# A place of its own for every gathered and result tile in the last stage of an expert layer, with deeper buffers around it

## What is computed

```python
gate_scores = softmax(x @ Wg.T)                      # x: 2048 tokens of 256
topk_val, topk_idx = top_k(gate_scores, 2)
topk_val = topk_val / (topk_val.sum() + EPS)
for e in range(8):
    a, b = split(x @ W1[e].T + b1[e])                # 2 x 512
    g = a * sigmoid(b)
    out = out + (g @ Wo.T + bo) * comb[..., e]       # comb: 2 of the 8 are not zero
x = x + out
```

## Time and profile before

| | us |
|---|---|
| runs without profile: median of 3 | 633.45 (632.12 to 635.2) |
| the profiled execution, its own time | 636.3 |
| its span, first to last instruction | 634.4 |
| first gather of the combination issued at | 569.75 |
| last addition begins at | 630.90 |

### The profile page before, as it was taken

How to read it: one execution, slowest core, us unless ns; L and a number is a source line. 1 busy time by engine, 2 the same in 40 slices (tenths; PEclk the granted TensorE clock), 3 DMA queues, 4 the chain that set the end, 5 groups by cost and what they waited for, 6 DMA issues and landing times. The chain is left out here.

```text
span 634.4 us, 21694 instructions
## 1 busy us (share of the span) xinstructions
PE 599.9 (95%) x8364; PEld 487.6 (77%) x8364; DVE 459.2 (72%) x1073; ACT 339.9 (54%) x743; POOL 330.7 (52%) x482
## 2 busy tenths in 40 slices
PE   9999999999999999999999999886999999997677
PEld 4788878888788887888886788663678888864456
DVE  3688867887778886777775855888799877763343
ACT  3677867888687886887772446441322333321111
POOL 3357858688587885788852332130422332207560
PEclk9999999999999999999999999896999999999798
DMA  9624644857255746965203991039334434427672
GB/s 244 148 67 108 185 153 123 240 164 226 93 190 162 209 134 190 232 186 168 72 3 105 429 368 34 34 112 385 126 126 136 139 125 137 129 93 208 165 227 63
DMA packets 65204, 102.10 MB, mean 161 GB/s; under 512 B 15408, under 2 KB 42096, under 8 KB 64080
## 3 DMA queue, kind: packets, MB, share of 16 engines
q1 hardware_dynamic: 59808, 86.42, 42.3%
q0 software_dynamic: 4432, 13.50, 7.7%
q10 hardware_dynamic: 864, 0.79, 0.5%
HBM read 69.42 MB, written 31.26 MB: 159 GB/s over the span
## 5 line engine op out<-in xcount | busy, mean ns | idle before, releaser
L537 DVE TENSOR_SCALAR Pm<-scores 128x514 f32<-128x514 f32 x128 | 88.1, 688 | 57.0 <-PE scores L750 56.8
L653 ACT ACTIVATE Pm<-Pm,nm 128x257 f32<-128x257 f32 x256 | 115.8, 505 | 2.5 <-DVE nm L542 2.5
L542 DVE TENSOR_REDUCE nm<-Pm 128x2 f32<-128x514 f32 x128 | 87.5, 684 | 2.2
L1634 POOL DMA_INDIRECT Xg<-y_d,inv x39 | 37.1, 951 | 87.2 <-PE scores L1819 69.9
L648 ACT ACTIVATE PT<-bank 128x512 f32<-128x512 f32 x64 | 38.2, 598 | 74.3 <-PE bank L761 74.3
L731 PE MATMUL bank<-hA,wH 128*128 128x258 f32 x256 | 75.4, 305 | 0.1
L738 PE MATMUL bank<-wH,hA 128*128 128x256 f32 x256 | 74.5, 302 | 0.5 <-DVE PT L549 0.5
L761 PE MATMUL bank<-cst,Pm 128*128 128x128 f32 x512 | 69.9, 279 | 0.0
L731 PE MATMUL bank<-hA,wL 128*128 128x258 f32 x256 | 69.1, 280 | 0.0
L738 PE MATMUL bank<-wL,hA 128*128 128x256 f32 x256 | 68.9, 280 | 0.0
L1834 PE MATMUL bank<-W,xh 128*128 x208 | 66.7, 402 | 1.0 <-DVE xl L1742 1.0
(11 more groups left out here) (262 smaller groups left out, 1449.2 us busy)
## 6 DMA issues: line engine op xcount, KB each, us to landing
w_d<-whl SPq DMA_DIRECT2D x64, 256.0 KB, 3.5
W<-w_d SPq DMA_DIRECT2D x8, 2048.0 KB, 15.5
g_d<-gg SPq DMA_DIRECT2D x39, 256.0 KB
wst<-in_W1T SPq DMA_DIRECT2D x32, 256.0 KB, 3.5
cx<-in_ctxT SPq DMA_DIRECT2D x31, 258.0 KB, 3.0
cx<-in_ctxT SPq DMA_DIRECT2D x62, 129.0 KB, 3.4
bb<-in_b SPq DMA_DIRECT2D x8, 512.0 KB
xb<-in_x SPq DMA_DIRECT2D x4, 512.0 KB, 4.6
```

The source lines that it names most:

```text
L537: v.tensor_scalar(Pm[:, i % 2, 2 * p:2 * p + 2, :], S4[:, 2 * p:2 * p + 2, 0:NK], -CLAMP, CLAMP, ALU.max, ALU.min).then_inc(s_cl, 1)
L542: v.tensor_reduce(nm[:, i % 2, 2 * p:2 * p + 2], Pm[:, i % 2, 2 * p:2 * p + 2, :], AX.X, ALU.max, negate=True).then_inc(s_nm, 1)
L653: a.activation(Pm[:, i % 2, g, :], Pm[:, i % 2, g, :], ACT.Exp, bias=nm[:, i % 2, g:g + 1]).then_inc(s_ex, 1)
L1634: g.indirect_dma_start(out=Xg[:, i % 3, :], out_offset=None, in_=y_d, in_offset=bass.IndirectOffsetOnAxis(ap=inv[:, i:i + 1], axis=0)).the ...
```

## The change

`cg` and `fo` get a place for each of the 16 tiles, and `zc` and `zT` get four in place of two. They lie where the expert weights were, which the first gather waits for in both kernels. The waits follow the new sizes:

```diff
-        area(27, 60)
-        cg = put("cg", [128, 4, 2, 512])
-        zc = put("zc", [128, 2, 512])
-        zT = put("zT", [128, 2, 512])
-        fo = put("fo", [128, 4, C])
+        area(27, 155)
+        cg = put("cg", [128, NTILE, 2, 512])
+        zc = put("zc", [128, 4, 512])
+        zT = put("zT", [128, 4, 512])
+        fo = put("fo", [128, NTILE, C])
...
                     if j >= 4:
-                        g.wait_ge(c_z, j - 3)
+                        g.wait_ge(c_g[j % 4], 32 * (j // 4))
...
             def final(v, j):
                 v.wait_ge(c_o, j + 1)
-                if j >= 4:
-                    v.wait_ge(c_out[j % 4], 32 * (j // 4))
...
-                    if j >= 2:
-                        v.wait_ge(c_t, j - 1)
+                    if j >= 4:
+                        v.wait_ge(c_t, j - 3)
...
-                    if j >= 2:
-                        final(v, j - 2)
-                final(v, NTILE - 2)
-                final(v, NTILE - 1)
+                    if j >= 4:
+                        final(v, j - 4)
+                for j in range(NTILE - 4, NTILE):
+                    final(v, j)
...
-                    if j >= 2:
-                        a.wait_ge(c_o, j - 1)
-                    a.activation(zT[:, j % 2, :], B[j % 2][:, :], ACT.Copy).then_inc(c_te, 1)
+                    if j >= 4:
+                        a.wait_ge(c_o, j - 3)
+                    a.activation(zT[:, j % 4, :], B[j % 4][:, :], ACT.Copy).then_inc(c_te, 1)
...
                 def back(j):
                     t.wait_ge(c_z, j + 1)
-                    if j >= 2:
-                        t.wait_ge(c_te, j - 1)
+                    if j >= 4:
+                        t.wait_ge(c_te, j - 3)
...
                 back(0)
+                back(1)
                 for j in range(NTILE):
-                    if j + 1 < NTILE:
+                    if j < NTILE - 4:
+                        back(j + 2)
+                    if NTILE - 4 < j < NTILE - 1:
                         back(j + 1)
```

More of the change, by code:

```diff
@@ L1622, in _ @@
                     for b in range(2):
-                        sp.dma_start(od[j, b], fo[64 * b:64 * b + 64, j % 4, :]).then_inc(c_out[j % 4], 16)
+                        sp.dma_start(od[j, b], fo[64 * b:64 * b + 64, j, :]).then_inc(c_out[j % 4], 16)
                 for s in c_out:
@@ L1642, in _ @@
                     if j >= 4:
-                        g.wait_ge(c_z, j - 3)
+                        g.wait_ge(c_g[j % 4], 32 * (j // 4))
                     for k in range(2):
-                        g.indirect_dma_start(out=cg[:, j % 4, k, :], out_offset=None, in_=g_d,
+                        g.indirect_dma_start(out=cg[:, j, k, :], out_offset=None, in_=g_d,
                                              in_offset=bass.IndirectOffsetOnAxis(ap=pi[:, k, j:j + 1], axis=0)
@@ L1671, in final @@
                 v.wait_ge(c_o, j + 1)
-                if j >= 4:
-                    v.wait_ge(c_out[j % 4], 32 * (j // 4))
-                v.tensor_tensor(fo[:, j % 4, :], B[4 + j % 4][:, 0:C], xb[:, j, :], ALU.add).then_inc(c_f, 1)
+                v.tensor_tensor(fo[:, j, :], B[4 + j % 4][:, 0:C], xb[:, j, :], ALU.add).then_inc(c_f, 1)
             @block.vector
@@ L1756, in _ @@
                     v.wait_ge(c_g[j % 4], 32 * (j // 4 + 1))
-                    if j >= 2:
-                        v.wait_ge(c_t, j - 1)
-                    v.tensor_scalar(zc[:, j % 2, :], cg[:, j % 4, 0, :], cmb[:, 0, j:j + 1], None, ALU.mult
+                    if j >= 4:
+                        v.wait_ge(c_t, j - 3)
+                    v.tensor_scalar(zc[:, j % 4, :], cg[:, j, 0, :], cmb[:, 0, j:j + 1], None, ALU.mult
                                     ).then_inc(c_m, 1)
                     v.wait_ge(c_m, j + 1)
-                    v.scalar_tensor_tensor(out=zc[:, j % 2, :], in0=cg[:, j % 4, 1, :], scalar=cmb[:, 1, j:j + 1],
-                                           in1=zc[:, j % 2, :], op0=ALU.mult, op1=ALU.add).then_inc(c_z, 1)
-                    if j >= 2:
-                        final(v, j - 2)
-                final(v, NTILE - 2)
-                final(v, NTILE - 1)
+                    v.scalar_tensor_tensor(out=zc[:, j % 4, :], in0=cg[:, j, 1, :], scalar=cmb[:, 1, j:j + 1],
+                                           in1=zc[:, j % 4, :], op0=ALU.mult, op1=ALU.add).then_inc(c_z, 1)
+                    if j >= 4:
+                        final(v, j - 4)
+                for j in range(NTILE - 4, NTILE):
+                    final(v, j)
             @block.scalar
@@ L1841, in back @@
                     t.wait_ge(c_z, j + 1)
-                    if j >= 2:
-                        t.wait_ge(c_te, j - 1)
+                    if j >= 4:
+                        t.wait_ge(c_te, j - 3)
                     for m in range(4):
-                        mm = t.transpose(B[j % 2][:, 128 * m:128 * m + 128], zc[:, j % 2, 128 * m:128 * m + 128], ident)
+                        mm = t.transpose(B[j % 4][:, 128 * m:128 * m + 128], zc[:, j % 4, 128 * m:128 * m + 128], ident)
                     mm.then_inc(c_t, 1)
@@ L1861, in _ @@
                     for m in range(4):
-                        mm = t.matmul(B[4 + j % 4][:, 0:C], zT[:, j % 2, 128 * m:128 * m + 128], WoT[:, m, :],
+                        mm = t.matmul(B[4 + j % 4][:, 0:C], zT[:, j % 4, 128 * m:128 * m + 128], WoT[:, m, :],
                                       start=(m == 0), stop=(m == 3))
```

## The result

The change makes the kernel slower: a median of 648.25 us (646.74 to 650.83, 4 runs) against 634.33 us (632.12 to 635.70, 4 runs) for the kernel before in the same comparison, a ratio of 1.0209 with a 95% interval of 1.0172 to 1.0246. The forecast was 623.5 and the range 619.5 to 631. It is rival D that came about: its span of 645.4 was met to within a microsecond, its time of 644.5 was 3.8 us under the median. The profiled execution took 646.74 us, the least of the four, with a span of 644.8.

A forecast was written before the change was run, and what follows sets the result against it. POOL's issue of gathers was taken as the slowest step, interrupted by waits for sums that late PE ends delayed. From 636.3 profiled, -12.9 + 3.0 = -9.9 gave 626.4, and 2.9 lower for plain runs 623.5 us; range 619.5 to 631.

The forecast's parts named there:

- rival D: Running gathers keep PE's ends back from about product 1 until 612.5; slower, 644.5 us; chance 0.13.
- Holds that stay: Late PE ends remain after the change, behind more buffers; cost +3.0 us at the end, with 0 and 6.5 as ends.
- holds: Ends of PE's work reaching other engines late, after PE's row ends; about 8.9 us at product 1, 4.0 at copy 11.
- the sum: Forecast total: end 12.9 us earlier, plus 3.0, makes -9.9 from the profiled 636.3; plain runs 2.9 lower, 623.5 us.
- The gathers' part: On POOL, the landing wait costs nothing and 32 gathers run without a gap; last issue ends 6.9 us earlier.
- The argument from the profiler: Plain runs' median is only 2.9 us below the profiled execution, so the late PE ends were taken as real.
- A: No late PE ends left, or none showing at the end: -12.9 us, 620.5 us; chance 0.25.
- B: Gather and store transfers become the bound, 240 or 213 GB/s: 622.5 to 628 us; chance 0.10 of over 627.5.
- C: Late PE ends grow with the unbroken run of gathers, eating most of the gain: 630 to 636 us; chance 0.09.
- Additions four behind: On DVE, addition j-4 behind sum j costs nothing more, with 0.9 us free for each tile.
- transpositions two ahead: On PE, product j stands behind transposition j+2 and ends a tile later; the later addition covers it, at no price.
- The slow start: After a pause PE runs at a lower clock, so its first product costs up to 1.7 us more.

The follow-up runs named there:

- e9: Changed kernel with POOL writing 256-float-wide zeros to unused SBUF behind each gather and waiting for it; 636.66 us, ratio 1.0009.
- e1: Changed kernel with the old wait put back: tile j's gathers wait for the sum of tile j-4; 636.32 us, ratio 1.0012.
- e3: Changed kernel with the 32 gathers replaced by plain transfers of consecutive rows issued by SP, same bytes; 618.12 us, one execution.
- e14: Changed kernel with each product cut into two halves of 128 columns, doubling its matrix instructions; 650.11 us, one run.
- e11: Changed kernel with POOL writing 16-float-wide zeros to unused SBUF behind each gather and waiting for it; 640.20 us, ratio 1.0039.

## Why the prediction was wrong

**The step that failed** is "Holds that stay": it took +3.0 us, with ends at 0 and 6.5. Without holds the sum's span is 634.4 - 12.9 = 621.5; the measured span is 644.8, so by the sum's own terms the holds cost 23.3. The gathers' part came true: 32 gathers without a gap, the last begun at 609.04 (near 609 forecast), the landing wait never binding, landings not slower (sum 5, the last sum that is not behind a held addition, begins at 587.43). The rest of the 12.9 the result can't test, as the holds cover it. The runs without holds put it a little lower: in e9 the end comes 13.8 us behind the begin of the last gather (621.40, span 635.2), where the sum had 621.5 - 608.9 = 12.6; by that the span without holds would be near 622.8 and the holds cost 22.

**Why it was taken too small.** I read the lengths of the holds, 9 and 4 us, as a property of PE that the change leaves alone ("The change takes none away; it puts more buffers behind them"). They were the lengths at which POOL's stop, or its last gather, had ended them. In the kernel before a hold makes a sum late, the late sum stops POOL (4.65 us), and the stop lets PE's ends through. e1 shows both halves: the wait alone, put back, gives the pauses and takes the loss away. The wait that looked like the bound was the brake that kept the real one short.

**Rival D** had the mechanism: a break in the gathers ends the hold; without it all ends from product 1 or so wait until 612.5, the end 32.9 us later, 645.4. Release came in steps (605.74, 613.44, 614.91), the span was 644.8. That the two agree so closely is in part luck: product 4 began 0.9 us after the 613.2 at which D has the work begin again, with a product and a transposition (2.2 us) fewer left than D counted. Its chance of 0.13 was cut by two rows that seemed to speak against it. Addition 4, let go after 1.07 us with gathers running, stands 7 us behind POOL's stop of 4.65 us; copy 11, let go after 4 us, is 1.6 us behind the last issue. The runs of gathers without a pause in which they stood were of at most six; the changed kernel makes one of 32.

**The argument from the profiler** ("I take them as real") was weak in its reason. The table of times before calls three runs "without profile", but every time in the results comes with a span, some 2 us below it, so no run here is known to be free of the recording. The holds cost time in all of these runs; whether they would without any recording is open.

**The rest.** A needed the holds to vanish. B took 240 GB/s for a bound: e3 moved 388 with plain transfers, so 240 was no bound of the DMA engines (for gathers no run tells, as POOL's issue paced them). C's first half (holds grow with the unbroken run) was right, its price too small. Additions four behind and transpositions two ahead cost and bring nothing that can be told (e1). The slow start of at most 1.7 us measured 1.9 (3.78 in place of 1.89).

**What stays open** is where in the chip an end waits. Shown is that the long remote waits are all for PE's work, that it takes indirect transfers issued at rests of 0.4 us or less, that it goes by instruction and not by bytes, and that in e14 PE's begins are held as well. The Trainium skill, Perfetto Trace Analysis, section Tensor Engine Instruction, says that the start is recorded when an instruction begins to read and that the end is estimated; the trace agrees, with ends up to 25.3 us ahead of their effect (product 2). The Trainium skill, NOTIFIC — the notification-queue block, section 7.1, says that the block which writes trace records holds its producers back inside rather than lose a record. If that is what happens here, the drip is one of the recording; no run here shows it or rules it out, as none is known to be free of recording.

## What to carry to other kernels

Before you take a wait away, ask what it gives the other engines while it lasts: here POOL's stop ended a stall on PE that the stop itself seemed unrelated to. Where the trace shows releases that come long after the row they wait for, find out what ends such a stall before you take its length for a constant; a length read under a feedback is not one. And price an operation's side effects from the longest unbroken run of it in the trace, not from shorter ones.

## What was not expected of the hardware

- While POOL issued indirect gathers at 1.25 us each (0.95 of issue, 0.30 of rest), PE's matrix instructions got through at 1.9 us each on average, where a row of them takes a quarter of a microsecond (eight in 1.89 us); the ends were seen up to 25 us behind their rows.
- 0.6 us of rest behind each gather took that away; 0.4 us put it off by some 17 us (first held: transposition 3, due at 585.7, in the changed kernel; product 6, due at 603.1, in e11).
- The same bytes by plain transfers, at up to 388 GB/s, did nothing to PE, whether SP or POOL issued them; half the bytes by gathers held it as long.
